# A two-layer cross-attention kernel on one core: 64 of 208 probability blocks turned by VectorE and sorted by DMA, and the norms' means from parted sums

## What is computed

```python
q, k, v = x @ w_q.T, ctx @ w_k.T, ctx @ w_v.T
x = x + alpha * (softmax(q @ k.T / sqrt(512)) @ v) @ w_o.T
def layer_norm(x, scale, offset):
    mu = mean(x, -1); var = var(x, -1)
    return (x - mu) * rsqrt(var + 1e-5) * scale + offset
for i in (1, 2):
    h = layer_norm(x, ln_scale[i], ln_offset[i])
    kh, vh = (ctx @ wk[i] + bk[i], bias_k[i]), (ctx @ wv[i] + bv[i], bias_v[i])   # 361 + 1 tokens
    x = x + (softmax((h @ wq[i] + bq[i]) @ kh.T / sqrt(128)) @ vh) @ wo[i] + bo[i]
h = layer_norm(x, ln_mlp_scale, ln_mlp_offset)
out = x + gelu(h @ w_fc1 + b_fc1) @ w_fc2 + b_fc2
```

## Time and profile before

| | before |
|---|---|
| median of 3 runs | 1784.99 us (1780.85 to 1785.19) |
| the profiled execution's own time | 1782.94 us |
| its span in the trace | 1781.1 us |
| PE busy | 1761.6 us, 99% of the span |
| DVE busy | 1155.0 us, 65% |
| POOL busy | 843.9 us, 47% |
| ACT busy | 745.3 us, 42% |

### The profile page before, as it was taken

The page is one execution under the profiler, slowest core; times in us unless marked ns, Lnnn a source line. Parts: engine busy times, 40 slices in busy tenths (PEclk is TensorE's granted clock), DMA queues, the critical chain, the costliest instruction groups (busy, mean ns, idle before and its releaser), DMA issues.

```text
span 1781.1 us, 30253 instructions
## 1 busy us (share of the span) xinstructions
PE 1761.6 (99%) x11146; PEld 1715.6 (96%) x11146; DVE 1155.0 (65%) x2705; ACT 745.3 (42%) x1624; POOL 843.9 (47%) x701
## 2 busy tenths in 40 slices
PE   8999999999999999999999999999999999999999
PEld 5899999999999999999999999999999999999999
DVE  3667676666876665657766566668766665676665
ACT  3634333333553333335443333345533333344554
POOL 2774342353584352534863423535834434315554
PEclk9999999999999999999999999999999999999999
DMA  9933231122551211223522211134412122104342
GB/s 261 246 119 86 68 94 40 35 81 81 137 143 35 56 54 52 79 62 99 142 78 52 80 40 56 54 107 123 135 36 62 44 58 80 58 22 142 112 137 78
DMA packets 116165, 156.90 MB, mean 88 GB/s; under 512 B 48344, under 2 KB 63960, under 8 KB 116020
## 3 DMA queue, kind: packets, MB, share of 16 engines
q1 hardware_dynamic: 113300, 150.68, 30.1%
q10 hardware_dynamic: 2720, 4.30, 0.8%
HBM read 149.81 MB, written 5.14 MB: 87 GB/s over the span
## 4 chain that ended last, share of the span: by engine, by line
PE 91%; DVE 4%; DMA 1%; POOL 1%; ACT 1%; issue 1%; SPq 0%; ACTq 0%; DVEq 0%; POOLq 0%
PE psum L695 28%; PE psum L697 28%; PE psum L696 28%; PE psum L1019 4%; PE psum L729 2%; DMA key_stage<-head_w_dram 1%; DVE prob L1826 1%; DVE centred L1729 0%; DVE a_lo L1525 0%; ACT prob L1372 0%; DVE stats L1817 0%; PE psum L708 0%; PE psum L866 0%; PE psum L704 0%; POOL x_held L651 0%
## 5 line engine op out<-in xcount | busy, mean ns | idle before, releaser
L555 POOL TENSOR_TENSOR wbuf_hi<-stage,zero_col 128x512 fp32r<-128x512 f32 x256 | 271.8, 1062 | 694.2 <-PE psum L697 497.0
L610 POOL TENSOR_TENSOR wbuf_lo<-stage,wbuf_hi 128x512 fp32r<-128x512 f32 x256 | 334.9, 1308 | 20.1
L695 PE MATMUL psum<-pT_hi,ctx_rows_hi 121*128 121x250 f32 (+3 forms) x1152 | 332.6, 289 | 0.0
L697 PE MATMUL psum<-pT_hi,ctx_rows_lo 121*128 121x250 f32 (+3 forms) x1152 | 331.3, 288 | 0.0
L696 PE MATMUL psum<-pT_lo,ctx_rows_hi 121*128 121x250 f32 (+3 forms) x1152 | 330.8, 287 | 0.0
L695 PE MATMUL psum<-ctxT_hi,a_hi 128*125 128x362 f32 (+1 forms) x832 | 280.8, 337 | 0.4
L697 PE MATMUL psum<-ctxT_hi,a_lo 128*125 128x362 f32 (+1 forms) x832 | 272.7, 328 | 0.0
L696 PE MATMUL psum<-ctxT_lo,a_hi 128*125 128x362 f32 (+1 forms) x832 | 272.5, 328 | 0.0
L1525 DVE TENSOR_TENSOR a_lo<-psum,a_hi 128x500 fp32r<-128x500 f32 (+2 forms) x288 | 144.2, 523 | 174.1 <-ACT a_hi L1147 174.0
L695 PE MATMUL psum<-a_hi,wbuf_hi 128*128 128x400 f32 x720 | 255.2, 354 | 1.6 <-DVE xT L1744 1.6
L697 PE MATMUL psum<-a_hi,wbuf_lo 128*128 128x400 f32 x720 | 247.6, 344 | 0.0
(11 more groups left out here) (197 smaller groups left out, 3450.0 us busy)
## 6 DMA issues: line engine op xcount, KB each, us to landing
stage<-head_w_dram SPq DMA_DIRECT2D x256, 256.0 KB, 2.8
mlp_stage<-mlp_w_dram SPq DMA_DIRECT2D x32, 512.0 KB, 3.6
ctx_rows_in<-ctx_dram SPq DMA_DIRECT2D x20, 726.0 KB
ctxT_in<-ctxT_dram SPq DMA_DIRECT2D x20, 724.0 KB, 6.9
p_b<-p_scratch SPq DMA_DIRECT2D x64, 200.0 KB, 3.6
key_stage<-head_w_dram SPq DMA_DIRECT2D x22, 256.0 KB, 8.5
l0w<-l_w_dram ACTq DMA_DIRECT2D x16, 256.0 KB, 9.1
x_held<-x_scratch SPq DMA_DIRECT2D x4, 800.0 KB, 5.7
```

The source lines that it names most:

```text
L555: return nc.gpsimd.tensor_tensor(out, in_, zero_col[0:in_.shape[0], :].broadcast_to(tuple(in_.shape)), ALU.add)
L610: nc.gpsimd.tensor_tensor(lo, held, hi.bitcast(F32), ALU.subtract).then_inc(stage_free, 1)
L695: pe.matmul(out, a_h, x_hi, start=start, stop=False)
L697: return pe.matmul(out, a_l, x_hi, start=False, stop=stop)
```

## The change

Three things change.

**Tokens in three full chunks.** The 362 tokens are padded to 384 (`W`), and a chunk of the token axis holds 128 tokens that are spread over it: partition 4i + g of chunk t is token 96g + 32t + i. The context rows are laid out so on the host. `exps` now works on 384 columns; the padding has scores of -1e30. For blocks that PE turns, `exps` reads the scores with the four groups innermost (`by_token`, a step of 96 columns) and writes `prob` in the order of the chunks.

**16 blocks of each phase in squares** (`in_squares`: x = 0 of units 0 to 4, except batches 0 and 1 of units 2 and 4). PE turns nothing for them. DVE turns `prob` in place in squares of 32 by 32 behind `normalise`; SP issues four transfers (`sort_squares`, 32 partitions to 128 partitions by 96 columns each) into one buffer `sorted0`; ACT and DVE make the halves of `pT` from that buffer; ACT's queue sends the first row from it in two transfers, without the copy on DVE. The sorts stand in SP's queue at `SORTED_AT`, and `exps` two blocks later waits for the sort instead of a transpose. Buffers shrink to make room (`P0_BUFS` 4 to 3, `ROW_BUFS` 3 to 2), and some late key loads of the first phase stand behind sorts.

**Means from parted sums.** POOL adds the chunks as before and then parts the sum in two halves (two more instructions), and PE makes each mean by two one-pass products. `hidden_variance` moves behind `scores(k, b, 1)`. In the MLP POOL adds the chunks too, and two products stand for eight, at later places; the third MLP load goes ahead of the load of `x_next`.

```diff
+def in_squares(k, b, x):
+    return k < len(UNITS) - 1 and x == 0 and not (k in LATE and b < 2)
...
+def sorted_behind(k, b, x):
+    done = len(pieces("start"))
+    for kk, bb in STEPS[:STEPS.index((k, b))]:
+        done += sum(len(pieces((kk, bb, place))) for place in "amb")
...
+    return done + WBUFS + 1
...
+            def sort_squares(ph, k, b, x):
+                at = k, b, x
+                n = sorted_blocks(ph, at)
+                sp.wait_ge(squares_turned, ph * Q_LAYER + Q_AT[at] + 1)
+                if n > 0:
+                    used_in, user = divmod(n - 1, len(BY_HELD[x]))
+                    sp.wait_ge(pt_lo, used_in * S_LAYER + T_AT[BY_HELD[x][user]] + 1)
+                    sp.wait_ge(p0_sent[x], 32 * n)
+                for a in range(GROUPS):
+                    squares = prob[a * SQUARE:(a + 1) * SQUARE, S_AT[at] % 2, :].rearrange("i (g f) -> i g f", g=GROUPS)
+                    sp.dma_start(held[x][:, a, :], squares).then_inc(sorted_ld[x], 16)
...
                 for i in range(early + 2 * (ph > 0), W_AT["v", H - 1]):
+                    for at in IN_SQUARES:
+                        if SORTED_AT[at] == i:
+                            sort_squares(ph, *at)
...
+            def part_sum(total, parts, done):
+                hi, lo = parts
+                pool.wait_ge(sum_step, done + DC - 1)
+                copy(hi, total).then_inc(sum_step, 1)
+                pool.wait_ge(sum_step, done + DC)
+                return nc.gpsimd.tensor_tensor(lo, total, hi.bitcast(F32), ALU.subtract)
...
+            def mean_of_parts(out, hi, lo):
+
+                pe.matmul(out, mean_r[:, :], hi, start=True, stop=False)
+                return pe.matmul(out, mean_r[:, :], lo, start=False, stop=True)
...
                 def turn_probs(k, b, x):
+                    if in_squares(k, b, x):
+                        return
...
                         run_pieces((k, b, "a"))
+                        scores(k, b, 1)
                         if (k, b) == VARIANCE_IN:
                             hidden_variance()
-                        scores(k, b, 1)
...
-                    nc.scalar.activation(prob[0:rows, i % 2, :], bank[S_BANK + i % 2][0:rows, 0:T], ACT.Exp,
-                                         bias=st[:, 0:1], accum_out=st[:, 2:3]).then_inc(s_exp, 1)
+                    out, scored = prob[0:rows, i % 2, :], bank[S_BANK + i % 2][0:rows, 0:W]
+                    if not in_squares(k, b, x):
+                        out, scored = by_chunk(out), by_token(scored)
+                    nc.scalar.activation(out, scored, ACT.Exp, bias=st[:, 0:1], accum_out=st[:, 2:3]).then_inc(s_exp, 1)
...
                 def probs_hi(k, b, x):
...
+                    if in_squares(k, b, x):
+                        act.wait_ge(sorted_ld[x], GROUPS * 16 * (sorted_blocks(ph, (k, b, x)) + 1))
+                        copy(in_columns(pT_hi[:, :, square_columns(k, x)]), held_chunks(x)).then_inc(pt_hi, 1)
...
                     nc.vector.tensor_scalar(prob[0:rows, i % 2, :], prob[0:rows, i % 2, :], st[:, 3:4], None, ALU.mult)\
                         .then_inc(s_norm, 1)
+                    if in_squares(k, b, x):
+                        dve.wait_ge(s_norm, ph * S_LAYER + i + 1)
+                        nc.vector.transpose(prob[:, i % 2, :], prob[:, i % 2, :]).then_inc(squares_turned, 1)
```

More of the change, by code:

```diff
@@ L160 @@
 P0_READ_AT = [max(made_before_turn(*LAST_BLOCK_OF[h]), W_AT["v", P0_FREED_BY[h]] + 1) + WBUFS for h in range(H)]
+def sorted_behind(k, b, x):
+    done = len(pieces("start"))
+    for kk, bb in STEPS[:STEPS.index((k, b))]:
+        done += sum(len(pieces((kk, bb, place))) for place in "amb")
+    if x == 1:
+        done += len(pieces((k, b, "a"))) + len(pieces((k, b, "m")))
+    elif k in LATE and b == 1:
+        done -= len(pieces((k, 0, "b"))) - 2
+    return done + WBUFS + 1
+SORTED_AT = {at: sorted_behind(*at) for at in IN_SQUARES}
+P0_READ_AT = [max(P0_READ_AT[h], SORTED_AT.get(LAST_BLOCK_OF[h], 0)) for h in range(H)]
 def build(nc, xT_d, ctxT_d, ctx_d, l0w_d, alpha_d, head_w_d, cols_d, rows_d, norm_d, mlp_w_d, mlp_b_d, out_d):
@@ L468, in load_first_probs @@
                 g = ph * H + VALUES.index(h)
[L469 to L470 removed]
+                until = T_AT[LAST_BLOCK_OF[h]]
+                copied = ph * PE_LAYER + sum(T_AT[at] <= until for at in BY_PE)
+                for s in range(max(copied - ROW_BUFS, 0), copied):
+                    sp.wait_ge(p0_out[s % ROW_BUFS], p0_written(s))
+                for j in range(HELD):
+                    wait(sp, p0_sent[j], 32 * (ph * len(BY_HELD[j]) + sum(T_AT[at] <= until for at in BY_HELD[j])))
                 wait(sp, p0_add, g - P0_BUFS + 1)
@@ L499, in _ @@
                 for i in range(early + 2 * (ph > 0), W_AT["v", H - 1]):
+                    for at in IN_SQUARES:
+                        if SORTED_AT[at] == i:
+                            sort_squares(ph, *at)
+                            for _ in range(LATE_KEYS_BEHIND_SORTED.get(at, 0) if ph == 0 else 0):
+                                load_late_key_weights(next(keys))
                     for h in VALUES:
@@ L633, in _, with add_chunks @@
             pool.wait_ge(kw_s, KEYS_BEFORE)
+            def add_chunks(chunks, total, done, c0, c1, from_use=None):
+                for c in range(c0, c1):
+                    if c > 1:
+                        pool.wait_ge(sum_step, done + c - 1)
+                    if from_use is not None:
+                        from_use(c)
+                    nc.gpsimd.tensor_tensor(total, chunks(0) if c == 1 else total, chunks(c), ALU.add).then_inc(sum_step, 1)
+            def part_sum(total, parts, done):
[4 more added lines that the diff above has]
+                return nc.gpsimd.tensor_tensor(lo, total, hi.bitcast(F32), ALU.subtract)
```

283 lines of the change are left out of this document (183 added, 100 removed).

## The result

The changed kernel takes 1771.4 us (median of 4 runs, 1768.7 to 1774.8), against 1785.1 us of the kernel before on the same chip: a ratio of 0.9925, 95% interval 0.9908 to 0.9942, so 13.7 us off. The profiled execution took 1768.73 us (span 1766.9), 14.2 us less than the 1782.94 of the one before. The forecast was 1764, with 1752 to 1777 as range: the time lies in it, 7 us above the forecast, or 5 us by the profiled execution, since the forecast was worked out from the profiled execution of the kernel before. The likeliest case's own range (1760 to 1770) does not hold it; it is nearest to the rival "waits take back half" with its 1772 us. What follows shows that the sum came out about right for reasons that partly cancelled.

The account below looks back on a forecast made before the run. PE was taken to bound the kernel, busy 1761.6 of 1781.1 us. Gains of 27.7 us less 6.2 (exponentials) and 1.8 (step (5, 2)) gave 19.7 off 1782.94, 1763.2, said as 1764 us; range 1752 to 1777.

Parts of the forecast that it names:

- likeliest case: Whole kernel: 1764 us, with its own range 1760 to 1770 us; chance 0.45.
- waits take back half: Rival, chance 0.12: load for v0 and sorts of (0, 3) and (3, 0) land late; 8 us in all, 1772 us.
- The gains from PE: Work taken off PE: 64 turns 21.1 us, last norm 4.7, hidden means 1.3, hidden variances 0.6; together 27.7 us.
- The norms: Products made one-pass or moved: last norm saves 4.7 us, hidden means 1.3, hidden variances 0.6.
- The sorts: At (0, 3): block sorted 5.3 us after its scaling, 6.6 us allowed, so sorts costed at nothing.
- the exponential: Reordered PSUM read costs 0.39 us more; 16 uncovered blocks at the ends of unit 5's steps lose 6.2 us.
- step (5, 2): Root on ACT waits for the variance, exponential is slower; PE loses 0.45 us four times, 1.8 us.
- The rival with 0.30: Chance 0.30: the exponential's strided read costs nothing, so its 6.2 us shrink to 0.3; 1756 us.
- Nothing lost, but it is the thinnest place: Step (1, 1), v0's load behind a sort on SP: DVE stands 5.2 us, 0.9 us left before PE's turn.
- DVE pays 0.45 us for each transpose ... on an engine with 600 us idle: DVE's transposes and low halves, less the saved row copy, add some 25 us, covered by its idle time.
- Everywhere else PE finds its data ready: Before the change, PE's listed waits were only 15, 6.1 us together, for DVE's scaling at unit 5's last blocks.
- some tenths: Single head: eight exponentials standing in its chain add some tenths of a us, taking 1763.2 to 1764 us.

## Why the prediction came out as it did

**Right.** *The gains from PE.* 432 transposes, 28 us less of PE's busy time (1.5 of them clock), and 0.33 us a turn: with the waits removed the squares brought 20 of the 21.1 us. *The norms.* 6.6 us were forecast for them all and 8 (6 to 11) measured; the last norm's products take 0.34 us each, 0.18 apart, and PE waits for no sum in the MLP. *The sorts.* They were costed at nothing, and no wait of PE leads back to a sort's own landing where I had placed the danger, at (0, 3): in the third phase ACT took that block 4.8 us after its scaling without waiting. Elsewhere ACT waited nine times for a sort, and in the 7 us behind each of these PE has no gap over 0.2 us. The parts of that chain were off in both directions, and cancelled: the transpose takes 0.58 us, not 0.45; the four issues 2.5 us, not 1.5; the landing 2.0 us, not 3.6. *DVE* grew by 29 us, forecast 25.

**Wrong, and cheaper than I said: the exponential (6.2 us) and step (5, 2) (1.8 us).** The step that failed here is "I take 0.39 us, by the row that it is nearest to". The nearest row was a strided write to SBUF; this is a strided read of PSUM, and it costs 0.001 us. The rival with 0.30 had it right. The Trainium skill (SBUF — State Buffer, "Door 1: The DMA port swizzle") has non-contiguous patterns in PSUM slow matmuls by its lines of 8 bytes; by 128 reads of ACT here at a step of 96 columns that does not carry over to ACT. Unit 5 as a whole lost 0.7 us.

**Wrong, and dearer: what stands behind whom.** Beyond those 8 us the prediction charged no wait at all, and 14.7 us came, 14.0 of them outside unit 5.
- *"Nothing lost, but it is the thinnest place"*, the turn of (1, 1, 1): 5.1 us. The chain was named link by link, and the place and the mechanism are right. The term was mis-sized: the fourth issue of the sort ends 2.5 us after the first begins, not 1.5, and the load is seen by DVE 4.3 us after its issue, not 3.6. With the transpose's 0.13 these 1.8 us exceed the 0.9 that were left. The issue's 0.38 us was the row of another kind of transfer.
- *"DVE pays 0.45 us for each transpose ... on an engine with 600 us idle"*: 4.3 us at the pieces o1 and o6. Idle time in total is not cover at a place. The prediction nowhere follows the additions to x, which stand directly behind a transpose in DVE's queue and whose banks PE takes up at once. Its sentence "Everywhere else PE finds its data ready" was too strong as well: of the 13.7 us that PE waits in the main loop before the change, 2.0 stand at o1 and o6 of the first phase, and four times 0.66 in front of the variance, for POOL.
- *Late keys*, 1.6 us: the diff moved their loads behind the sorts, and the prediction never priced it. With one load moved the gap fell from 2.1 to 0.4.
- *The start and the single head*, 2.9 us where I allowed some tenths. Of it 1.4 stand at 64.6 us, behind DVE's low half of the context columns; 1.3 are loads at the start, which vary between executions.
- *The lock between DVE and POOL* is in none of the terms. It was there before the change, 22 times, and the change shifts which scalings meet a POOL instruction. The Trainium skill (SBUF — State Buffer, "Who interferes with whom") states it: a DVE operation in a two-port mode and a POOL instruction exclude each other for the whole instruction, a scaling (`tensor_scalar`) can enter such a mode unless it also writes its accumulator, and a DVE operation with two SBUF operands contends with a POOL instruction that reads SBUF. The traces agree: 43 scalings end 0.21 to 0.22 us behind POOL, 5 of the 64 low halves from the sorted buffer are prolonged, by 0.5 us on average, where those from PSUM never are, and in the accumulating form not one of 208 is.

The rival "waits take back half" had the time, 1772 us, but only part of the reason. PE did wait 1.0 to 1.8 us in step (1, 1); yet the load of v0 landed 3.6 to 4.2 us after its issue, before the change 3.1 to 3.6, and not 2 us later, and the sorts of (0, 3) and (3, 0) cost nothing. That its 8 us stand close to the measured time is chance.

The forecast of the whole owes as much to luck. It was missed by 5.5 us (19.7 against 14.2 off the profiled execution), or by 7.0 without the 1.5 us of clock. Behind that stand two larger errors of opposite sign: 7.3 us of costs that did not come, and 14.0 us of waits that nobody had charged, 6.7 us between them.

Open: why one sort kept ACT waiting for 2.8 us was not followed up, and the loads at the start and the clock were not separated from the change by an experiment.

## What to carry to other kernels

Cover is local: for an instruction put into a queue, follow the one directly behind it to who waits for that, and price the chain with the issue cost of its own kind of transfer. Where a bound engine has lost N us of work and the time falls by less, list its gaps beyond the usual pitch by place; here each place had its own cause, and three small changes of order gave back 15 us. When an instruction is long only now and then, look at what ends just before it does. And before a microsecond or two between two traces is put down to a change, hold their granted clocks against each other stretch by stretch.

## What the runs showed of the hardware

- A plain scaling of 384 fp32 columns on DVE, SBUF to SBUF, takes 0.42 us; 43 of 208 that met a POOL instruction ended 0.21 to 0.22 us after that one and took up to 1.30 us. With an accumulator output all 208 take 0.61 us, and 0.08 more for reading the accumulator.
- It works the other way too: a POOL instruction of 1.3 us took 2.77 us beside DVE's low half of the context columns, which has two SBUF operands.
- A transpose in squares of 128 x 384 fp32 on DVE takes 0.578 us, 64 times within 2 ns, 13 of them begun with more than 0.65 us of a POOL instruction still ahead.
- ACT's exponential of 384 columns takes 579.5 ns read in order and 580.9 ns read one column in 96 from PSUM.
- An issue of a transfer from 32 to 128 partitions, 48 KB, takes SP 0.60 us in the median, and lands after 2.0 us; over 256 of them the landing took 1.95 to 3.97 us.
- Where the granted clock of TensorE was 1.2 GHz, one-pass products of 400 columns started 0.33 us apart, at 2.4 GHz 0.18 us.
